# A graph kernel: picks with the edge pieces held still, sums for the scales on ScalarE, and the unrolled path placed first

## What is computed

```python
# layer 0, twice, with W0, b0 and W1, b1
neigh = segment_sum(x[cols] / degree[rows], rows)        # rows = src, cols = dst
x1 = relu(concat([x, neigh], axis=1) @ W.T + b)
x = layernorm(x + x1)
# layer 1
h_self, h_neigh = x @ W_self, x @ W_neigh
h_sparse = h_neigh where it is among the 32 largest of its row, else 0
neigh = segment_sum(h_sparse[src], dst) / max(degree, 1)
out = layernorm(x + h_self + neigh)
```

## Time and profile before

| | us |
|---|---|
| median of three runs | 713.2 |
| the profiled execution | 714.56 |
| its span | 712.8 |
| TensorE busy | 641.9 |
| VectorE busy | 512.7 |
| ScalarE busy | 341.1 |

### The profile page before, as it was taken

One profiled execution on the slowest core, in us unless ns is written; L12 is line 12 of the kernel. 1 busy time (PEld: TensorE's weight loads), 2 busy tenths in 40 slices (PEclk: granted clock), 3 DMA queues, 4 the chain that ended last, 5 costly groups with the idle time before them and its releaser, 6 DMA issues.

```text
span 712.8 us, 11318 instructions
## 1 busy us (share of the span) xinstructions
PE 641.9 (90%) x3987; PEld 347.3 (49%) x3988; DVE 512.7 (72%) x1306; ACT 341.1 (48%) x657; POOL 109.8 (15%) x190
## 2 busy tenths in 40 slices
PE   4918788888887999999999999999999979999996
PEld 3717566666643444444444444444444434444443
DVE  6579988999937787888885467878778853734433
ACT  4318878999947576777765233333333320100000
POOL 4000222222210001010110122232323200000000
PEclk9999999999998999999999999999999999999999
DMA  9413454545540011111110366555554504310000
GB/s 212 85 45 97 149 177 152 164 155 159 156 148 22 29 39 35 39 34 43 31 44 23 109 177 186 154 182 167 167 177 154 166 18 138 116 54 24 22 25 27
DMA packets 39543, 73.09 MB, mean 103 GB/s; under 512 B 3120, under 2 KB 32207, under 8 KB 39481
## 3 DMA queue, kind: packets, MB, share of 16 engines
q1 hardware_dynamic: 39481, 72.30, 34.1%
HBM read 38.91 MB, written 33.38 MB: 101 GB/s over the span
## 4 chain that ended last, share of the span: by engine, by line
PE 70%; DVE 19%; ACT 4%; DMA 3%; issue 2%; SPq 1%; POOL 0%; DVEq 0%; ACTq 0%; POOLq 0%
PE pair L1510 35%; PE bank L1600 9%; PE pair L1600 8%; DVE hots L632 7%; PE bank L1400 7%; PE pair L1400 4%; PE bank L1392 2%; DVE ct L775 2%; ACT own L1083 2%; PE pair L1293 2%; DVE x_t L768 1%; PE bank L1406 1%; DMA w_nat<-in_L_gnn_W_dram 1%; DMA own_in<-own_dram 1%; ACT x_t L1076 1%
## 5 line engine op out<-in xcount | busy, mean ns | idle before, releaser
L1510 PE MATMUL pair<-xs,ct 125*128 125x512 f16 x625 | 147.1, 387 | 0.0
L1510 PE MATMUL pair<-a,ct 125*128 125x512 f16 x625 | 142.8, 379 | 0.0
L632 DVE TENSOR_TENSOR hots<-iota,jobs 128x1792 f16<-128x1792 f16 (+1 forms) x100 | 104.2, 1061 | 4.6 <-issue 3.9
L1510 PEld LDWEIGHTS pair<-xs,ct 125*128 125x128 f16 x625 | 62.2, 101 | 70.9 <-issue 5.7
L1510 PEld LDWEIGHTS pair<-a,ct 125*128 125x128 f16 x625 | 61.0, 99 | 68.1
L1065 ACT ACTIVATE slab<-pair 125x875 f16<-125x875 f32 (+1 forms) x100 | 83.7, 861 | 20.5 <-PE pair L1369 19.1
L1187 ACT ACTIVATE a<-ct 125x1000 f16<-125x1000 f16 (+1 forms) x75 | 80.2, 1069 | 8.4 <-DMA c_dram<-slab 7.5
L1600 PE MATMUL bank<-xs,ct 125*128 125x512 f16 (+1 forms) x325 | 71.5, 379 | 0.0
L1600 PE MATMUL pair<-xs,ct 125*128 125x512 f16 x300 | 66.4, 379 | 0.0
L1369 PE MATMUL pair<-hots 128*128 128x125 f16 x625 | 54.2, 228 | 12.4 <-ACT slab L1065 7.4
L1392 PE MATMUL bank<-ident,slab 125*128 125x125 f16 x625 | 52.6, 223 | 12.9 <-DVE ct L775 10.9
(11 more groups left out here) (199 smaller groups left out, 859.6 us busy)
## 6 DMA issues: line engine op xcount, KB each, us to landing
c_dram<-slab SPq DMA_DIRECT2D x25, 683.6 KB
ct<-c_dram SPq DMA_DIRECT2D x25, 683.6 KB
own_in<-own_dram SPq DMA_DIRECT2D x50, 125.0 KB
own_dram<-own SPq DMA_DIRECT2D x25, 125.0 KB
own_dram<-own_st SPq DMA_DIRECT2D x25, 125.0 KB
x_in<-in_x_dram SPq DMA_DIRECT2D x25, 125.0 KB
z_dram<-z_st SPq DMA_DIRECT2D x25, 125.0 KB
a<-z_dram SPq DMA_DIRECT2D x5, 625.0 KB
```

The costliest lines, as they stand in the source:

```text
L632: v.tensor_tensor(hots[k][:, :, :, :].rearrange("p w g (a d) -> p (w g) a d", d=2), iota, job, ALU.is_equal).then_inc(win_hot, 1)
L1510: ins = mm(agg[k % 3][0:lhs.shape[1], :], lhs, parts[l][:, t, :], start=t == 0, stop=t == NT - 1, skip_group_check=True)
```

## The change

The gather of the picks swaps its operands: the pieces (now three columns wider, filled with zeros) are stationary and `pick` streams, in two parts of 320 and 305 windows with two blocks of 125 slots each. The result then has slots on partitions and windows in the free dimension, which is the layout of `jobs`; so the transposes of columns (1303) and VectorE's copy (640) go, and ScalarE writes `jobs` from `row_key` and `row_src` in SBUF. The window number is subtracted by one product over a row of ones.

VectorE's reductions of absolute maxima go. ScalarE squares x (in four parts), both layer-1 weights and the bias, with a sum along the row, takes the square roots and writes them to `stat`. The first two parts of x stand ahead of its load of `matched`, the rest between the copies of tile 0. The factor in the bound of the sparse part goes from 1.01 to 1.43, the floor of the bounds from 1e-20 to 1e-13.

The scales' steps move into tiles 1 and 2: on TensorE `bounds_t` behind the second transposes of tile 1, `bounds_row` behind its last fill, `scales_b` behind the first fill of tile 2. On VectorE `bound_rows` stands behind all four hots of tile 1, `bounds` behind the first hots of tile 2, `scales_out` behind its second. The clearing of the transposes' banks moves ahead. The first two high halves of the weights move on ScalarE from tile 1 to tile 2. Three sets of tile 0's hots stand ahead of the count and the fourth behind it.

The quick path's block now stands first on all three engines, the general path's second.

In a tile that follows one with two own products, VectorE's low half for the next product no longer ends the tile before but stands behind the first hots; TensorE's first half of that product stands behind the first transposes and no longer ahead of them.

```diff
-PICKS = [(0, 2), (2, 4), (4, 5)]
-PITCH = 256
+PICKS = [(0, 320), (320, QN)]
...
+        both = [t[:, :, :].rearrange("p (b w) c -> p b (w c)", b=2) for t in pair]
...
             def unpack(k):
 
                 lo, hi = PICKS[k]
                 dve.wait_ge(row_copied, k + 1)
-                step(v.scalar_tensor_tensor(held_row[:, lo:hi, :], row[:, lo:hi, :], float(PACK * PACK - PACK), row[:, lo:hi, :],
+                step(v.scalar_tensor_tensor(held_row[:, :, lo:hi], row[:, :, lo:hi], float(PACK * PACK - PACK), row[:, :, lo:hi],
                                             ALU.is_lt, ALU.mult))
-                step(v.tensor_tensor(fold[:, lo:hi, :], held_row[:, lo:hi, 0:QS], held_row[:, lo:hi, QS:PITCH], ALU.add))
-                step(v.tensor_scalar(row_key[:, lo:hi, :], fold[:, lo:hi, :], 1.0 / PACK, -0.49, ALU.mult, ALU.add))
-                step(v.tensor_scalar(row_key[:, lo:hi, :], row_key[:, lo:hi, :], ROUND, -ROUND, ALU.add, ALU.add))
-                v.scalar_tensor_tensor(row_src[:, lo:hi, :], row_key[:, lo:hi, :], -float(PACK), fold[:, lo:hi, :],
+                step(v.tensor_tensor(fold[:, lo:hi], held_row[:, 0, lo:hi], held_row[:, 1, lo:hi], ALU.add))
+                step(v.tensor_scalar(row_key[:, lo:hi], fold[:, lo:hi], 1.0 / PACK, -0.49, ALU.mult, ALU.add))
+                v.tensor_scalar(row_key[:, lo:hi], row_key[:, lo:hi], ROUND, -ROUND, ALU.add, ALU.add).then_inc(cols_ready, 1)
+                dve.wait_ge(cols_ready, 2 * k + 1)
+                v.scalar_tensor_tensor(row_src[:, lo:hi], row_key[:, lo:hi], -float(PACK), fold[:, lo:hi],
                                        ALU.mult, ALU.add).then_inc(cols_ready, 1)
-                step(v.tensor_scalar(row_hit[:, lo:hi, :], row_key[:, lo:hi, :], 1.0, None, ALU.min))
-                v.tensor_reduce(hits[:, k:k + 1], row_hit[:, lo:hi, :].rearrange("p g s -> p (g s)"), X, ALU.add
-                                ).then_inc(count_ready, 1)
...
-            largest_x(0)
             unpack(0)
             unpack(1)
-            unpack(2)
-            dve.wait_ge(cols_t, 3)
-            v.tensor_copy(jobs[:, 4 * P:QN, :, :].rearrange("p w g d -> p g w d"),
-                          bank[0][:, 0:2 * P].rearrange("p (g w o) -> p g w o", g=2, o=1).broadcast_to([QS, 2, P, 2])
-                          ).then_inc(cols_copied, 1)
             dve.wait_ge(const_ready, NCONST)
-            dve.wait_ge(cols_copied, 3)
-            quick_hots(0, 0)
+            dve.wait_ge(cols_copied, 2)
+            for k in range(FILLS - 1):
+                quick_hots(0, k)
             dve.wait_ge(counted, 1)
             v.tensor_copy(matched[:, :], bank[1][0:1, 0:1]).then_inc(matched_ready, 1)
+            dve.wait_ge(cols_copied, 4)
+            quick_hots(0, FILLS - 1)
...
+            with dve.If(total > E - 1):
+                quick_hots(1, 0)
+                clear_tr()
+                for k in range(1, FILLS):
+                    quick_hots(1, k)
+                bound_rows()
+                for t in range(1, NT):
+                    more, own = t + 1 < NT, OWN[t]
+                    if more:
+                        quick_hots(t + 1, 0)
+                    if t == 1:
+                        bounds()
+                    if len(OWN[t - 1]) > 1:
+                        own_low(OWN[t - 1][1] + 1)
+                    tr_copy(t - 1, 1)
+                    if 1 < t < 5:
+                        w_low(2 * t - 4)
+                    if more:
+                        quick_hots(t + 1, 1)
+                    if t == 1:
+                        scales_out()
+                    if 1 < t < 5:
+                        w_low(2 * t - 3)
+                    if t == 2:
+                        own_low(0)
+                    if own and own[0] + 1 < NT:
+                        own_low(own[0] + 1)
+                    if more:
+                        quick_hots(t + 1, 2)
+                        quick_hots(t + 1, 3)
+                    tr_copy(t - 1, 3)
...
-                quick_hots(1, 0)
-                bound_rows()
-                clear_tr()
-                quick_hots(1, 1)
-                bounds()
-                quick_hots(1, 2)
-                scales_out()
-                quick_hots(1, 3)
-                for t in range(1, NT):
-                    more, own = t + 1 < NT, OWN[t]
-                    if more:
...
-                    if len(own) > 1:
-                        own_low(own[1] + 1)
...
+            def slots_out(k):
+                lo, hi = PICKS[k]
                 act.wait_ge(picked, k + 1)
-                a.activation(row[:, lo:hi, 0:2 * P], bank[1 + k][0:P, 0:(hi - lo) * 2 * P].rearrange("p (i c) -> p i c", c=2 * P),
+                a.activation(row[:, :, lo:hi], both[1 - k][0:P, :, 0:hi - lo],
                              ACT.Relu, bias=shift128[:, :], scale=float(PACK ** 2)).then_inc(row_copied, 1)
+
+            def jobs_out(k):
+                lo, hi = PICKS[k]
+                for g, m in ((1, row_key), (0, row_src)):
+                    act.wait_ge(cols_ready, 2 * k + 2 - g)
+                    a.activation(jobs[:, lo:hi, g, :], m[:, lo:hi].rearrange("p (w o) -> p w o", o=1).broadcast_to([QS, hi - lo, 2]),
+                                 ACT.Copy).then_inc(cols_copied, 1)
+
+            def square_x(c):
+                act.wait_ge(x_loaded[c], BOTH)
+                if c:
+                    act.wait_ge(squared, c)
+                n = (XC[c + 1] - XC[c]) * F
+                a.activation(slab[1][:, 0:n], xs32[:, XC[c]:XC[c + 1], :].rearrange("p t f -> p (t f)"), ACT.Square, scale=TINY,
+                             accum_out=squares[0:P, c:c + 1]).then_inc(squared, 1)
+
+            def square_weights():
+                act.wait_ge(eye_added, 2)
+                act.wait_ge(wn_loaded, 16)
+                act.wait_ge(b_loaded, 16)
+                for k, (m, n) in enumerate(((ws_nat[:, :, :].rearrange("p c f -> p (c f)"), 2 * F),
+                                            (wn_nat[:, :, :].rearrange("p c f -> p (c f)"), 2 * F), (bcol[:, :], 2))):
+                    act.wait_ge(squared, 4 + k)
+                    a.activation(junk[:, 0:n], m, ACT.Square, scale=TINY, accum_out=squares[:, 4 + 2 * k:5 + 2 * k]).then_inc(squared, 1)
+
+            def roots():
+                act.wait_ge(squared, 7)
+                a.activation(norms[:, :], squares[:, :], ACT.Sqrt).then_inc(rooted, 1)
+                act.wait_ge(rooted, 1)
+                a.activation(stat[:, 0:4], norms[:, 0:4], ACT.Copy, scale=1.0 / TINY).then_inc(stat_ready, 1)
+                a.activation(stat[:, 10:16], norms[:, 4:10], ACT.Copy, scale=1.0 / TINY).then_inc(stat_ready, 1)
...
+            slots_out(0)
+            jobs_out(0)
+            slots_out(1)
+            jobs_out(1)
             for l in range(2):
                 for h in range(2):
                     weights_out(l, h)
+            act.wait_ge(act_step, 4)
+            act.wait_ge(const_ready, 17)
+            square_x(0)
+            square_x(1)
...
             def quick_copies():
-                for f in range(FILLS):
-                    quick_copy(0, f)
+                quick_copy(0, 0)
+                square_x(2)
+                quick_copy(0, 1)
+                square_x(3)
+                quick_copy(0, 2)
+                square_weights()
+                roots()
+                quick_copy(0, 3)
                 for t in range(1, NT):
                     if t == HELD:
                         act.wait_ge(w_stored, 32)
                     own = OWN[t]
                     quick_copy(t, 0)
                     tr_copy(t - 1, 0)
+                    if t == 2:
+                        ready_for_own()
+                        w_high(0)
+                        w_high(1)
...
             for k, (lo, hi) in enumerate(PICKS):
-                for i in range(lo, hi):
-                    out = bank[1 + k][0:P, (i - lo) * 2 * P:(i - lo + 1) * 2 * P]
-                    mm(out, group_p[:, :], group_i[:, i, :], start=True, stop=False, skip_group_check=True)
+                for blk in range(2):
+                    out = both[1 - k][:, blk, 0:hi - lo]
+                    mm(out, ones_row[:, :], minus_row[:, lo:hi], start=True, stop=False, skip_group_check=True)
                     for g in range(EQ):
-                        if i == 0:
+                        if k == 0 and blk == 0:
                             pe.wait_ge(pick_ready, g + 1)
                             pe.wait_ge(pieces_ready, 2)
+                        at = (g + blk) * P
                         for n, m in enumerate((quint, piece[:, 0], piece[:, 1])):
-                            last = mm(out, pick[:, g, i * P:(i + 1) * P], m[:, g * P:(g + 2) * P],
+                            last = mm(out, m[:, at:at + 128], pick[:, g, lo:hi],
                                       start=False, stop=g == EQ - 1 and n == 2, skip_group_check=True)
                 last.then_inc(picked, 1)
...
```

(19 more changed lines are left out.)

171 lines of the change are left out of this document (62 added, 109 removed).

## The result

| | kernel before | changed kernel |
|---|---|---|
| median of the runs | 712.0 us (4 runs, 710.7 to 713.5) | 719.6 us (4 runs, 718.5 to 721.5) |
| profiled execution | 714.56 us, span 712.8 | 719.17 us, span 717.4 |
| ratio | | 1.0116, 95% interval 1.0082 to 1.0149 |

The change makes the kernel 7.6 us slower by the medians and 4.6 us slower by the two profiled executions; that of before lies 2.5 us over its median, that of after 0.4 under its own. In a later batch the changed kernel stood at 1.0134 (1.0105 to 1.0163).

The account below looks back on a forecast made before the run. VectorE was taken to set the count stage's 5.7 us tiles, with changes before 203.4 us reaching the end one to one. Terms +3.0 + 3.3 - 1.1 + 3.7 = +8.9 us gave 722.0 us on the median, range 715.5 to 726.0.

Parts of the forecast that it names:

- Start-up, +3.0: Setup and first tiles: ScalarE's squares and the moved scales put VectorE's hots (2,2) at 61.5 instead of 58.5, +3.0 us.
- Picks, -0.4 at the last pick: Setup: one group less puts the last pick at 29.5 instead of 29.85; first hots at 33.5, before 33.73.
- Double tiles, +1.1 each: After tiles 6, 8, 10: VectorE's later low half costs +1.1 us a pair, +3.3; ScalarE's shorter store stop gives -1.1.
- The drop of the clock: Granted clock falling to 0.51 from 104.3 us: one drop left in the sum; it may vanish, -1.7 us.
- The jump, +3.7: End of count stage: TensorE's jump over the general path, without cover, delays the next stage's first product, +3.7 us.
- VectorE covered: End of count stage: VectorE's jump is hidden, its first sum tree being wanted only after TensorE's 50 products.
- The cheap jump (718.3): Rival: the sequencer makes the jump while the last transposes still wait, saving 3.7 us: 718.3, chance 0.17.
- The later low half for nothing (719.8): Rival: the hots are done before the low half is wanted, so it costs nothing: 719.8, chance 0.11.
- More half clock after the jump (724 to 726): Rival: more windows of half clock at the new waits or after the jump, +2 to +4 us, chance 0.08.
- The case of no difference: Rival: tile 1's lead of 3.8 us pays the jump of 3.7, the rest cancels: 713.1 to 716, chance 0.13.
- The faster case: Rival: VectorE has slack in early tiles, deciding where its work falls below about 5.4 us: 709.3, -3.9, chance 0.06.
- The sign named for being wrong: Prediction wrong if the next stage's first product starts before 208 us or no 3.8 us TensorE branch precedes it.

Follow-up runs that it names:

- squares_short: Changed kernel with each ScalarE square of x taking only its first tile (256 elements instead of 1536 or 1792): 717.8 us, 1.0083.
- quick_first_on_before: Kernel before with only the order of the quick and general blocks turned, on all three engines: 714.1 us, 1.0046.
- picks_alone: Kernel before with the changed kernel's picks, quick block first and the first 50 products of the next stage inside both blocks: 707.4 us, 0.9955.
- no_general_pe: Changed kernel without TensorE's instructions for the general path: 712.2 us, 1.0021.
- sums_inside: Changed kernel with TensorE's first 50 products of layer 0 moved into both blocks, ahead of its jump: 713.1 us, 1.0050.
- before_sums_own_late: Kernel before with quick block first, first 50 products inside both blocks, and the changed kernel's order of own products and low halves: 708.7 us, 0.9963.
- general_first: Changed kernel with the general path's block ahead of the quick path's again on all three engines: 715.8 us, 1.0080.
- pe_general_first: Changed kernel with the general path's block first again on TensorE alone: 715.3 us, 1.0063.

## Why the prediction was right, and where its steps were not

The forecast of 722.0 us stands against 719.6, in the range and in the likeliest case's own; slower by more than 0.5% came true. The sum of +8.9 us stands against +7.6 by the medians. The mechanisms were the right ones: the squares stand ahead of ScalarE's copies, the low half comes later, the jump moves to where TensorE has no cover. That the number is so near is partly luck: the start-up was taken 2.9 us too long and the jump 2.6 us too short, and these two errors cancel.

**Start-up, +3.0: the profile has +0.1.** The mechanism was the right one. ScalarE's squares eat what the earlier fills give (squares_short gives 4.25 of it back, quick_first_on_before shows 2.9 us gained with no squares), and VectorE waits for the sums. The sizes were too big along the row. The weights were out at 35.4, not 36.7, as the picks were early; two squares were done at 38.7, not 40.1; and tile 0 was out at 48.1, not 50.4. From there on the forecast nearly held: TensorE turned the sums 2.0 us later (50.14), where I had 2.1, and the serial steps began 2.4 us behind that (52.57), where I had 2.9. They took 2.5 us, the spread came 2.9 us behind them (57.98), and hots (2,2) 0.6 later, all as forecast. The whole row is 2.9 us early at its end, 2.3 of it at tile 0. Two figures of the prediction don't follow from what stands beside them: the 0.82 ns an element (the two squares, of 1792 and 1536 elements, took 1.69 and 1.48 us and bear it out), and tile 1's lead, 3.8 and 4 us there, which by its own 54.99 and 50.4 is 4.6. Measured, tile 1's first copy was 6.9 us ahead (48.1), and none of it was left at tile 3.

**Picks, -0.4 at the last pick and 33.5 at the first hots: 32.09.** The first hots came 1.6 earlier than before, 1.4 earlier than forecast. The last pick was out at 28.11, not 29.5: the product that subtracts the window's number now runs at 11.62, while TensorE still waits for `pick`, and the first product over `pick` starts at 13.95 instead of 14.70; the prediction had not counted this. Part of the rest is chance (31.7 to 33.7 with the old picks). Worth at the end: nothing measurable in picks_alone.

**Double tiles, +1.1 each: +0.7.** The place was right, TensorE's wait of 1.43 us for the low half and VectorE's 1.73 behind it. I had 1.8 for TensorE's wait and a low half 1.4 us later; behind hots of 1.08 us, not 1.37, it was 1.0 later. With the stop: -0.7 where I had -1.1. The drop of the clock that I left in the sum was gone in both profiles of the changed kernel, the alternative named there (-1.7). In net the six tiles are 0.2 us shorter than before instead of 2.2 longer. Why a low half 1.0 later costs 0.7 and not more was not taken apart.

**The jump, +3.7: +6.3, and slow products behind it.** This is the term that carried the result. That it is not gone but moved, and that TensorE has no cover there, was right, and no_general_pe and sums_inside show it. Its size was taken from the start, 3.79 us. Behind the last transposes it took 6.41, 7.11, 6.41, 6.95 and 7.08 us in five profiles with that order and transfers running, above the upper bound of 5 that the prediction gave, 4.71 with the slab's store held back, and 3.35 to 3.79 in seven profiles where it lies at the start or behind products. That the slab's store would lengthen it was foreseen, the amount was not. The term also lacks what follows the idle stretch: in all six profiles that have it the first 50 products took 12.57 to 13.75 us, the changed kernel's 12.98, where 10.96 is the time at full clock.
The Trainium skill (Runtime: NRT & Kernel Launch, section Instruction fetch mechanics) says that a taken branch whose target is not in the two pages held makes the engine fetch the target's page by a DMA first. The trace agrees in that the branch is gone when there is nothing to skip (no_general_pe) and is longer the more transfers run beside it (the table above). The section gives no duration for it.

**VectorE covered: nearly.** Its jump shows as 6.64 us of issue ahead of the first sum tree in the changed kernel. It was hidden there only because TensorE came 6.3 late. ScalarE's (6.68 us of issue, and a table load of 1.28 behind it) costs little: its first work of the stage begins at 211.91, and before it waited for the slab's store until 211.13. Where TensorE is on time, VectorE's 7.5 to 8.2 us let the degrees' product wait 0.8 to 1.5.

**Rivals.** The cheap jump (718.3) is refuted by the rows. The later low half for nothing (719.8) gave nearly the measured time for the wrong reason. More half clock after the jump (724 to 726) was there as a mechanism, some 2 us against full clock, but not in the total. The case of no difference is out by the interval (1.0082 at the least). The faster case failed where it was said to decide: late tiles stay at 5.67 us. The sign named for being wrong did not come: the first product starts at 209.7, behind the bound of 208, if ahead of the 212 forecast.

By the medians the parts come to this, each from two kernels that differ in it: blocks turned, +3.5 us (quick_first_on_before; -2.9 at the start, +6.9 at the end); own products, +1.2 (before_sums_own_late); picks, +0.6 (picks_alone), no difference that can be told from nothing; squares on ScalarE with the scales in tile 1, sums_inside less picks_alone and less the own products, 0.0095 or 6.8 us less 1.2, so +5.5. They add up to 10 to 11 us against the 8 to 9.5 measured in two batches. Each is uncertain by some 2 us, so the sum agrees; only the order of the sizes is shown. What the stop for the weight parts takes from whatever comes early is in each of them.

## What to carry to other kernels

A block that is skipped is paid for where the jump is made: turning the order of two blocks moves the price, and it is worth it only where the engine has work queued ahead of the jump to run meanwhile, as the 50 products written into both blocks were (0.9947 against 1.0046 for the turned blocks alone). Before work is moved to an engine off the critical path, lay out that engine's row up to the next thing the others wait for: 6 us of squares taken from a waiting VectorE stood ahead of ScalarE's copies, which everyone needed. And a lead won ahead of a wait for a store can end at that store (2.9 of 4.25 us in squares_short).

## What was not expected of the hardware

- A taken branch over TensorE's general block took 3.3 to 3.8 us at the start or behind queued products, 4.7 with fewer transfers, 6.4 to 7.1 with the slab's store and loads running. Behind the idle stretch the granted clock was 0.50 for the first products, which made 50 of them 1.6 to 2.8 us longer than the 10.96 at full clock. On VectorE and ScalarE the branch's own row is short (73 and 50 ns at 203 us and the time shows as issue ahead as issue ahead of the next operation (6.64 and 6.68).
- The picks have two paces. In the profile of general_first (first row below), 23 products of TensorE started between 17 and 20 us, in that of the changed kernel 13, with the same shapes, the same granted clock in the row and the same DMA share:

```profile
17.00:20.00 3.00, 3.00 (x23) 1.91 (x21) 0.80 (x1) 0.80 (x1) 0.00 (x0) 1.00 1.13 220
```

```profile
17.00:20.00 3.00, 3.00 (x13) 1.41 (x12) 0.00 (x0) 0.00 (x0) 0.00 (x0) 1.00 1.13 230
```

A product of 320 columns took 0.30 us there and 0.44 here, and the next one started 0.14 us later against 0.27 (2.3 columns a ns against 1.2, about the ratio of the clock's two levels). The count was known some 5 us earlier. It is the one execution of 14 profiled that did so, and in pe_general_first and picks_alone a granted clock of 0.50 at 17 to 20 us went with the slow pace just the same (12 products). So the granted clock of 1.00 in these rows does not tell which pace the picks have. What sets it is open. It can explain single runs that are 5 us faster (704.1 among 17 of the kernel before with a median of 709.9), but this was not tried.
